# A macaron block (experts, state-space scan, experts): the order of work on both sides of the scans, split gathers, and two steps of scan 0 moved to GpSimd

## The reference

```
x = x + 0.5 * ffn(layernorm(x))
x = x + ssm(layernorm(x))
x = x + 0.5 * ffn(layernorm(x))        # same weights

ffn(x):  logits = x @ router_w                          # 8 experts
         e = argmax(logits); s = sigmoid(max(logits))
         out[t] = (silu(s*x[t] @ gate_w[e]) * (s*x[t] @ up_w[e])) @ down_w[e]
         out += (silu(x @ sh_gate) * (x @ sh_up)) @ sh_down      # every token
ssm(x):  dt_x, B, C = split(x @ W_x.T, [64, 16, 16]); dt = softplus(dt_x @ W_dt.T + b_dt)
         h[t] = exp(dt*A) * h[t-1] + dt*B*x;  y[t] = sum over 16 states of h*C;  y += x * D
```

## Time and profile before

| what | us |
|---|---|
| median of 3 runs (lowest, highest) | 548.02 (545.97, 550.7) |
| the profiled execution, its own time | 548.89 |
| its span, first to last instruction | 547.2 |
| busy: PE, DVE, ACT, POOL | 442.1 (81%), 342.6 (63%), 261.0 (48%), 277.4 (51%) |
| mean granted TensorE clock, of full speed | 0.921 |

### The profile page before, as it was taken

One profiled execution on the slowest core, in us unless ns is written; L12 is line 12 of the kernel. 1 busy time (PEld: TensorE's weight loads), 2 busy tenths in 40 slices (PEclk: granted clock), 3 DMA queues, 4 the chain that ended last, 5 costly groups with the idle time before them and its releaser, 6 DMA issues.

```text
span 547.2 us, 7087 instructions
## 1 busy us (share of the span) xinstructions
PE 442.1 (81%) x2236; PEld 308.7 (56%) x2236; DVE 342.6 (63%) x557; ACT 261.0 (48%) x499; POOL 277.4 (51%) x213
## 2 busy tenths in 40 slices
PE   1988899998777675796888688699789937999991
PEld 1855455554434465775775677689546523555550
DVE  5357244333665989998999899969757321333430
ACT  1200233331063899699899989767011001333330
POOL 6003266664120476688997989799200003466632
PEclk9869999999897999799799889879979985999997
DMA  8942022210410122131232133223041113132300
GB/s 291 383 123 65 21 77 62 67 47 20 153 60 0 42 77 78 59 108 49 91 100 94 44 101 100 83 62 104 1 136 58 54 63 82 57 93 84 112 30 8
DMA packets 33331, 45.69 MB, mean 84 GB/s; under 512 B 5258, under 2 KB 22478, under 8 KB 33296
## 3 DMA queue, kind: packets, MB, share of 16 engines
q1 hardware_dynamic: 28144, 34.70, 19.9%
q0 software_dynamic: 5152, 10.54, 6.6%
HBM read 37.33 MB, written 12.48 MB: 91 GB/s over the span
## 4 chain that ended last, share of the span: by engine, by line
PE 55%; DVE 23%; issue 9%; POOL 7%; ACT 3%; DMA 1%; DVEq 0%; POOLq 0%
PE bank L656 17%; DVE hs L1057 12%; PE bank L630 11%; PE bank L684 7%; PE bank L615 6%; POOL gs L378 3%; PE bank L770 3%; PE bank L585 2%; PE bank L753 2%; DVE stats L861 2%; DVE dbx_t L1041 2%; PE bank L672 2%; PE bank L667 2%; POOL xn_no L339 2%; PE bank L570 1%
## 5 line engine op out<-in xcount | busy, mean ns | idle before, releaser
L378 POOL TENSOR_TENSOR gs<-hs,c_sb 128x1024 f32<-128x1024 f32 x62 | 147.2, 2389 | 57.1 <-DVE hs L1057 50.6
L1057 DVE TENSOR_TENSOR_SCAN hs<-da,bank 128x1024 f32<-128x1024 f32 x64 | 145.1, 2277 | 4.7 <-PE bank L753 4.5
L753 PE MATMUL bank<-ident,dbx_t 128*128 128x128 f32 x512 | 74.0, 292 | 35.5 <-DVE hs L1057 32.4
L347 POOL DMA_INDIRECT da<-rows,row_token x46 | 47.3, 1029 | 102.2 <-DMA rows<-x_sb 55.9
L656 PE MATMUL bank<-w_gu,tt 128*128 x184 | 94.6, 638 | 3.9 <-ACT tt L434 3.9
L476 ACT ACTIVATE da<-dt_sb,a_neg 128x511 f32<-128x511 f32 x128 | 84.9, 712 | 13.8 <-DVE hs L1057 13.7
L753 PEld LDWEIGHTS bank<-ident,dbx_t 128*128 128x128 f32 x512 | 61.1, 150 | 49.3 <-DVE hs L1057 43.4
L490 ACT ACTIVATE dbx_t<-dtx_t,h_sb 128x256 f32<-128x256 f32 x194 | 83.7, 495 | 4.7 <-DVE dtx_t L1026 3.4
L967 DVE SCALAR_TENSOR_TENSOR q_sb<-th,bank 128x256 f32<-128x256 f32 x46 | 19.4, 421 | 103.4 <-ACT th L429 103.4
L770 PE MATMUL bank<-ident,gs 128*128 128x128 f32 x496 | 71.5, 292 | 8.2 <-POOL gs L378 8.0
L429 ACT ACTIVATE th<-bank,da 128x256 f32<-128x256 f32 x46 | 21.8, 474 | 102.8 <-PE bank L656 102.8
(11 more groups left out here) (118 smaller groups left out, 506.3 us busy)
## 6 DMA issues: line engine op xcount, KB each, us to landing
c_sb<-c_dram SPq DMA_DIRECT2D x64, 256.0 KB, 3.1
rows<-xn_no SPq DMA_DIRECT2D x8, 516.0 KB, 6.1
x_sb<-in_x SPq DMA_DIRECT2D x4, 512.0 KB, 6.4
w_gu<-in_gate_w SPq DMA_DIRECT2D x2, 1024.0 KB, 10.1
w_gu<-in_up_w SPq DMA_DIRECT2D x2, 1024.0 KB, 11.2
w_dn<-in_down_w SPq DMA_DIRECT2D x2, 1024.0 KB, 10.5
xn_no<-token_out SPq DMA_DIRECT2D x4, 512.0 KB, 6.3
rows<-x_sb SPq DMA_DIRECT2D x4, 512.0 KB, 3.5
```

Source lines behind the costliest of these rows:

```text
L347: nc.gpsimd.indirect_dma_start(out=xr[:, u, 0:WIDE[r]], out_offset=None, in_=rows[r], in_offset=bass.IndirectOffsetOnAxis(ap=row_token[:, ...
L378: nc.gpsimd.tensor_tensor(gs[:, s % 2], hs[:, s % RING], c_sb[:, s % RING].unsqueeze(1).to_broadcast([P, KC, L]), ALU.mult).then_inc(sc_g, 1)
L753: mm = nc.tensor.transpose(DBX[s % 2][:, k, i * P:(i + 1) * P], dbx_t[:, s % TURNS, i, k * P:(k + 1) * P], ident[:])
L1057: nc.vector.tensor_tensor_scan(hs[:, s % RING].rearrange(flat), da[:, s % RING].rearrange(flat), DBX[s % 2][:, :, :].rearrange(flat), 0.0, ...
```

## The change

It does the following, by place.

- XR is 7; BY_DVE of batch 3 and ROUTES are other values; three of the four route calls of run 1 stand in scan 3.
- Before the scans: the order of statistics, combines and normalisations on VectorE; normalise(1,2) on GpSimd; both shared_gate_up of batch 3 together, the second with its own banks and its hidden rows in y_sb's memory; shared_down(0,3), the transposes of batch 1's second half, and project(1) between turn_dbx calls and in the first scan step; its two shared_result halves after scan steps 1 and 2.
- In scan 0: combine(3) on GpSimd after product 4, rstd and normalise(1,3) there after product 9. Projection steps of batch 1 one state later, project(2) earlier.
- In scan 3: normalise(2,2) on VectorE. The last product but one on GpSimd, the last on VectorE in two halves.
- Behind the scans: the order of the shared expert, its down product into YA, count and sequence in other banks.
- Run 1's rows: SyncE writes the normalised rows to rows[0] and to rows[1], x_sb to rest and to rows[1]. The first seven tiles gather from rows[0], and later from rest; the others from rows[1]. result(0) to result(6) wait for the second gather.

```diff
...
-    XR = 6
+    XR = 7
...
-      + ((1, 1, 2, 1, 1, 1, 1, 1, 0, 1, 1, 1, 1, 0, 1, 1),))
-    ROUTES = (5, 10)
+      + ((1, 1, 2, 1, 1, 1, 1, 0, 1, 1, 1, 0, 1, 1, 1, 1),))
+    ROUTES = (4, 8, 13)
...
 def shared_banks(r, b, fo):
...
-    return (H[0], H[1]) if fo == 0 or (r, b) == (0, BATCH - 1) else (T, Y)
+    return (H[0], H[1]) if fo == 0 else (YS[0], YS[1]) if r == 1 or b == 3 else (T, Y)
...
+def hidden_rows(r, b):
...
+    return sg_h if (r, b) == (0, 3) else sh_h[:, b % 2]
...
+def shared_out(r, q):
...
+    return YA[q % 2] if r == 1 or q // 2 == 3 else YS[q % 2]
...
     def xn_rows(r):
...
-            sp.dma_start(row_tiles[r][:, rows_of(b), 0:D + 2], xn_no[:, rows_of(b), :]).then_inc(xn_out, 16)
+            sp.dma_start(row_tiles[0][:, rows_of(b), :], xn_no[:, rows_of(b), :]).then_inc(xn_out, 16)
+        for b in range(BATCH if r == 1 else 0):
+            sp.dma_start(row_tiles[1][:, rows_of(b), 0:D + 2], xn_no[:, rows_of(b), :]).then_inc(rows_full, 16)
...
     def rest_rows(b):
...
-        sp.dma_start(row_tiles[1][:, rows_of(b), D + 2:], x_sb[:, rows_of(b), :]).then_inc(rest_out, 16)
+        sp.dma_start(rest_tiles[:, rows_of(b), :], x_sb[:, rows_of(b), :]).then_inc(rest_out, 16)
+        sp.dma_start(row_tiles[1][:, rows_of(b), D + 2:], x_sb[:, rows_of(b), :]).then_inc(rows_full, 16)
...
     def experts(r):
...
-        def gather(j):
+        def gather(j, lo, hi, source, done):
...
-                out=xr[:, u, 0:WIDE[r]], out_offset=None, in_=rows[r],
+                out=xr[:, u, lo:hi], out_offset=None, in_=source,
...
-                bounds_check=TOK - 1, oob_is_err=False).then_inc(ff_in[u], 16)
+                bounds_check=TOK - 1, oob_is_err=False).then_inc(done[u], 16)
...
+        for j in range(XR):
+            gather(j, 0, WIDE[0], rows[0], ff_in)
+        if r == 1:
...
-        for j in range(XR):
-            gather(j)
+            for j in range(XR):
+                gather(j, WIDE[0], WIDE[1], rest, rest_in)
+            pool.wait_ge(rows_full, 16 * 2 * BATCH)
...
-                gather(j + XR)
+                gather(j + XR, 0, WIDE[r], rows[r], ff_in)
...
+    def combine(b):
+        pool.wait_ge(sh_x, LT // 2 * (b + 1))
+        pool.wait_ge(back_in[b], 16)
+        tiles = slice(LT * b, LT * (b + 1))
+        nc.gpsimd.tensor_tensor(x_sb[:, tiles], xn[:, tiles], x_sb[:, tiles], ALU.add).then_inc(back_x, 1)
...
     def scan(b):
...
-            if last_two(s):
+            if last_one(s):
...
-            if n == 3:
-                if b == 0:
-                    rstd_of(1, BATCH - 1)
-                else:
-                    rstd_of(2, b - 1)
+            if b == 0 and n == 4:
+                combine(BATCH - 1)
+            if b == 0 and n == 9:
+                rstd_of(1, BATCH - 1)
+                normalise(1, BATCH - 1)
+            if b > 0 and n == 3:
+                rstd_of(2, b - 1)
+                if b < BATCH - 1:
...
+    normalise(1, BATCH - 2)
...
     experts(1)
-    for u in range(4):
-        pool.wait_ge(ff_out[u], 16 * uses(u) * RUNS)
...
-            if more and n == 0:
+            if b == 1 and n == 0:
+                ln_copy(1, 7)
+            if more and b != 1 and n == 0:
...
-            if more and n in (1, 2):
-                project_abs(b + 1, n - 1)
-            if more and n == 3:
+            late = int(b == 0)
+            if more and n in (1 + late, 2 + late):
+                project_abs(b + 1, n - 1 - late)
+            if more and n == 3 + late:
...
-            if more and n == 4:
+            if more and n == 4 + late:
...
-            if n in (13, 14):
-                ln_copy(*((1, 6 + n - 13) if b == 0 else (2, 2 * (b - 1) + n - 13)))
+            if b == 0 and n == 14:
+                project_copy(2)
+            if b == 0 and n == 15:
+                ln_copy(1, 6)
+            turn = 13 if more else 10
+            if b > 0 and n in (turn, turn + 1):
+                ln_copy(2, 2 * (b - 1) + n - turn)
...
-    shared_tanh(0, 3, 0)
+    project_ln(0)
+    for fo in range(KC):
+        shared_tanh(0, 3, fo)
...
-    project_ln(0)
-    shared_tanh(0, 3, 1)
-    ln_copies(1, 2)
...
-    for s in range(AHEAD):
+    ahead(0)
+    ln_copy(1, 4)
+    for s in range(1, AHEAD):
...
+    ln_copy(1, 5)
...
+    for fo in range(KC):
+        shared_tanh(1, 0, fo)
+    shared_tanh(1, 1, 0)
...
     route(1)
-    for b in range(BATCH):
+    shared_tanh(1, 1, 1)
+    for b in range(2, BATCH):
...
     routed(1)
...
-                pe.wait_ge(pj_dtx, 4)
+                pe.wait_ge(pj_copy, 3)
...
     def route(r, b):
...
-            pe.wait_ge(sc_dve, states_by("dve", min(N * (BATCH - 1) + (ROUTES + (N, N))[b] + 3, STATES)))
+            pe.wait_ge(sc_dve, states_by("dve", min(N * (BATCH - 1) + (ROUTES + (N,))[b] + 3, STATES)))
...
-    def shared_down(r, b):
+    def shared_down(r, b, halves=(0, 1)):
...
-        if b == 0:
-            pe.wait_ge(rt_read, r + 1)
+        if (r, b) == (0, 0):
+            pe.wait_ge(rt_read, 1)
...
-        for q in range(2 * b, 2 * b + 2):
-            if q >= 2:
+        if (r, b) == (0, 3):
+            pe.wait_ge(pj_dtx, 2)
+        elif (r, b) == (1, 0):
+            pe.wait_ge(sc_x, KC * BATCH)
+        for q in (2 * b + h for h in halves):
+            if q >= 2 and (r, b) != (0, 3):
...
-                    last = nc.tensor.matmul(YS[q % 2][:, i * D:(i + 1) * D], sh_h[:, b % 2, k, t * P:(t + 1) * P],
+                    last = nc.tensor.matmul(shared_out(r, q)[:, i * D:(i + 1) * D], hidden_rows(r, b)[:, k, t * P:(t + 1) * P],
...
     def shared_gate_up(r, b, fo):
-        if b > 0:
-            pe.wait_ge(sh_hidden, 2 * (BATCH * r + b - 1) + fo + 1 + (fo if (r, b) == (0, BATCH - 1) else 0))
+        if (r, b, fo) == (0, 3, 1):
+            pe.wait_ge(sh_x, 6)
+        elif (r, b) == (1, 0):
+            pe.wait_ge(sc_h, STATES - 1 + fo)
+        elif b > 0:
+            pe.wait_ge(sh_hidden, 2 * (BATCH * r + b - 1) + fo + 1)
...
-    def shared(r, batches):
...
     def routed(r):
...
-            pe.wait_ge(ln_xnT, (GT // 2 + 6, GT, GT + 2)[b - 1])
+            pe.wait_ge(ln_xnT, (GT // 2 + 6, GT // 2 + 6, GT + 2)[b - 1])
...
+        if (b, k) == (2, 0):
+            pe.wait_ge(ln_xnT, GT)
...
-            pe.wait_ge(sh_hidden, 2 * BATCH)
+            pe.wait_ge(sh_hidden, 7)
...
-            pe.wait_ge(sh_x, GT // 2)
+            pe.wait_ge(sh_hidden, 8)
...
     def add(s):
...
-        products = gs
-        if last_two(s):
-            products = last
-            pe.wait_ge(sc_last, s - (STATES - 3))
-        else:
-            pe.wait_ge(sc_g, s + 1)
...
-            pe.wait_ge(pj_dtx, 2)
+            pe.wait_ge(sh_x, GT // 2)
...
+        if not last_one(s):
+            pe.wait_ge(sc_g, s + 1)
...
+            if last_one(s):
+                pe.wait_ge(sc_last, k + 1)
+            products = last if last_one(s) else gs[:, s % 2]
...
-                mm = nc.tensor.matmul(YA[k][:, i * P:(i + 1) * P], products[:, s % 2, k, i * P:(i + 1) * P], ident[:],
+                mm = nc.tensor.matmul(YA[k][:, i * P:(i + 1) * P], products[:, k, i * P:(i + 1) * P], ident[:],
...
+            if s == 0:
+                shared_down(0, 3, (1,))
+                ln_transposes(1, 5)
+                project(1)
+            if last_one(s):
+                shared_gate_up(1, 0, 0)
...
-            if more and n in (0, 1):
-                project_z(b + 1, n)
+            late = int(b == 0)
+            if more and n in (late, late + 1):
+                project_z(b + 1, n - late)
...
-            if n in (12, 13):
-                ln_transposes(*((1, 6 + n - 12) if b == 0 else (2, 2 * (b - 1) + n - 12)))
-            if n == N - 1 and b + 2 < BATCH:
+            turn = 12 if more else 9
+            if b > 0 and n in (turn, turn + 1):
+                ln_transposes(2, 2 * (b - 1) + n - turn)
+            if (b, n) in ((0, 13), (1, N - 1)):
...
+            if b == 0 and n in (14, 15):
+                ln_transposes(1, n - 8)
...
     route(0, BATCH - 1)
-    shared(0, 2)
+    count(0)
+    shared_gate_up(0, 0, 1)
+    shared_gate_up(0, 1, 0)
+    shared_down(0, 0)
+    sequence(0)
+    shared_gate_up(0, 1, 1)
+    shared_down(0, 1)
     routed(0)
...
-    shared_gate_up(0, 3, 0)
-    ln_batch(1, 1)
...
-    shared_gate_up(0, 3, 1)
-    ln_batch(1, 2)
-    shared_down(0, 3)
+    for fo in range(KC):
+        shared_gate_up(0, 3, fo)
+    ln_transposes(1, 2)
...
-    for s in range(2):
-        turn_dbx(s)
-    project(1)
+    ln_transposes(1, 3)
+    turn_dbx(0)
+    ln_transposes(1, 4)
+    turn_dbx(1)
+    shared_down(0, 3, (0,))
...
-    pe.wait_ge(sc_h, STATES)
-    route(1, 2)
-    shared_gate_up(1, 0, 0)
-    ln_batch(2, BATCH - 1)
+    shared_gate_up(1, 0, 1)
+    shared_gate_up(1, 1, 0)
+    ln_transposes(2, 6)
+    shared_down(1, 0, (0,))
+    ln_transposes(2, 7)
+    shared_down(1, 0, (1,))
     route(1, BATCH - 1)
-    shared(1, BATCH)
+    shared_gate_up(1, 1, 1)
+    count(1)
```

(85 more changed lines are left out.)

## The result

| | before | after |
|---|---|---|
| median (lowest, highest), us | 548.1 (545.97, 550.7), 4 runs | 515.64 (514.57, 515.98), 4 runs |
| profiled execution, its span | 548.89, 547.2 | 515.98, 514.3 |
| mean granted TensorE clock | 0.921 | 0.953 |
| busy PE, DVE, ACT, POOL, us | 442.1, 342.6, 261.0, 277.4 | 429.1, 339.3, 260.1, 292.7 |

The ratio is 0.9402 (95%: 0.9359 to 0.9446). The forecast was 514.2. The total came out near it by luck in part: the largest wrong term, 5.9 us, was offset by four small ones the other way, so the parts are what to read.

The account below looks back on a forecast made before the run. VectorE was taken to bound scan 0, TensorE the stretch behind the scans, work order the transition between. +0.4 - 8.7 - 0.9 - 21.7 - 3.8 = -34.7 us from 548.89 gave 514.2, range 505 to 526.

Parts of the forecast that it names:

- the 8.7: Transition and scan 0, up to scan 18: 8.7 us gained, scan 18 starting at 234.8 against 243.50.
- less some 8.5 of waits, 5.3 for ScalarE and 3.2 for GpSimd: Up to scan 18: waits taken off the 14 us earlier start plus 3.25 of VectorE's net work, leaving 8.7.
- the early lead is eaten by ScalarE: Rival, up to scan 18: only VectorE's lighter work gains, 0 to 4 us; total 519 to 523; chance 0.18.
- Scan 0's norm on GpSimd: Normalise(1,3) behind GpSimd's product 9: rstd 1.2 plus 4.84 us, products 10 to 15 then at 2.34 each.
- Scan 3: Batch 2's normalisation moves from GpSimd to VectorE, bank waits go, route calls fit beside scans: -0.9 us.
- the long figure: Scan 3: the moved normalisation costs VectorE 3.41 us beside products, taken as 3.4, rather than 1.37.
- Behind the scans: TensorE's shared work ends 46.0 us after the last scan, one idle piece of 1.1 us; first expert transpose 21.7 us earlier.
- the second rival: The join does not close: late residual gather or low TensorE clock behind the scans; 520 to 524 us; chance 0.17.
- The gather and the clock: Run 1's first tiles: no gather wait; without the gap, 3.19 us per tile at once, saving 3.8 us.
- T+57: Run 1's fourth tile: result(0) comes 57 us after the last scan's end; the residual gather lands at T+54.7.
- the 2.3 us of the prediction: Run 1's first tiles: spare time between the residual gather's landing and result(0).
- The 0.4 of the memset: Start: seven slots instead of six lengthen GpSimd's first memset, VectorE waits behind it: +0.4 us.

Follow-up runs that it names:

- run 1: Not a follow-up run: the kernel's own routed-expert pass behind the scans, 23 tiles, whose rows are gathered; no separate measured time.
- The old front kernel: Changed kernel with the transition into the scans and scan 0 as in the kernel before; 519.67 us, ratio 0.9476.
- the order alone: Kernel before with only scan 3 and the order behind the scans changed, one gather per tile in run 1; 530.41 us, ratio 0.9698.
- The one-gather kernels: Changed kernel, run 1 gathering whole rows once after all of x_sb is written; 525.04 us, ratio 0.9559; again on another chip 525.27, ratio 0.9605.
- the one with the transposes ahead: Changed kernel with the LayerNorm 1 transposes ScalarE waits for put ahead of turn_dbx(0) and turn_dbx(1); 510.24 us, ratio 0.9283.
- the split alone: Kernel before with only the split gathers and seven slots; 534.37 us, ratio 0.9748.

## Why the prediction was right, and where it was not

*The front: the 8.7 was mis-sized.* It measured 2.8 us in the profile, 2.5 to 4.1 by the experiments. The prediction called itself wrong where scan 18 moves by much other than 8.7, and in this term it was wrong. The first scan's lead was right (168.22 for 169.0; 12.9 us once run 0's 1.9 is taken off, for 14). The step that failed is "less some 8.5 of waits, 5.3 for ScalarE and 3.2 for GpSimd". From the first scan to scan 18 VectorE waited 14.2 us (1.6 in the kernel before). The part behind GpSimd's block was right, 3.3 us (2.29, 0.60 and 0.45); the part ahead of it measured 10.9 (2.06, 0.99, 2.91 and 4.94). I had named the two transposes that ScalarE waits for, but priced them at 1.4 and 3.7 with TensorE at its full clock. They cost 2.93 and 5.63, since the down product half between them took 3.44 instead of 1.89, turn_dbx(0) 1.94 instead of 1.07, and the transposes behind it 1.06 instead of 0.60: with the 1.22 instead of 1.07 of turn_dbx(2) this low clock, for which the forecast had no term, is 3.0 of the 3.5 us that the two waits were too long. A third wait was missing in the forecast, 4.94 for the turn of B (1.42 before). In TensorE's queue it stands behind the second z product (which waited 1.23 for ScalarE's late copy), a turn of dbx, an add and the skip product. Moving the transposes ahead gave back 7.8 us in the profile. That shows that the order of the queue was the cause, in part by way of the clock. The rival "the early lead is eaten by ScalarE" priced this stretch at 0 to 4 us, and 2.8 came; but ScalarE did not set the pace by its own work, it stood 8.6 us for the two transposes. Its total, 519 to 523, did not come, since the other terms made up for the front.

*Scan 0's norm on GpSimd.* The timeline of GpSimd, answering to the earlier trace rows:

```profile
194.05 2.19 POOL L393 TENSOR_TENSOR x_sb<-xn_no,x_sb 128x1024 f32<-128x1024 f32 x1
...
215.06 4.83 POOL L355 TENSOR_SCALAR xn_no<-x_sb,mv,rstd 128x256 f32<-128x256 f32 x4
```

It took 4.83 us for 4.84, the combine 2.19 for 2.4, with one wait of 2.29 and two short ones behind it. Its price was predicted rightly, though not how it comes about: the prediction let the products follow at 2.34 us each, and it came to TensorE's low clock (1.97 and 1.92 us at 222.26 and 224.02) after the 3.03 us that TensorE stood for the block. That the move made no difference against VectorE was not said. That the block can be cut up at the same work of GpSimd, and that this with the earlier statistics pays 4.4 us, was in no rival.

*Scan 3: better than predicted.* 2.2 us for 0.9. The old front kernel has the changed scan 3 and reaches T 327.37 us after F against 329.10 before: 1.7; with the order alone it is 2.4. The waits for banks in scans 1 to 3 fell from 4.5 us to 0.44, for 2.4 us more of VectorE's work (136.3 busy for 133.9). The normalisation took less than the long figure:

```profile
351.46 2.73 DVE L935 TENSOR_SCALAR xn_no<-x_sb,mv,rstd 128x256 f32<-128x256 f32 x4
...
354.98 2.29 DVE L1119 TENSOR_TENSOR_SCAN hs<-da,bank 128x1024 f32<-128x1024 f32 x1 [0.44 <-PE bank L791]
```

The Trainium skill's page "SBUF — State Buffer" ("Who interferes with whom") makes the two engines take turns by whole instructions, and the trace agrees: of the four instructions one took 1.76 us, from 351.46 to just behind the end of GpSimd's product at 353.07, and the others 0.40. In the 3.41 of before, one took 2.46 and the others 0.39 to 0.40. So what this work costs beside products is what is left of one product when it starts; the prediction had only the two totals.

*Behind the scans: right.* 46.93 us for 46.0, with the one idle piece of 1.1 us where it was put (1.08 before 388.07). The granted clock of 1.00 in all 33 us closes the second rival: the 0.74 of before did not belong to this work. In the kernel before TensorE had been busy 10.6 of the 15 us ahead of it, and had stood 1.68 us just before. The Trainium skill's page "TensorE: Matmul & The Clock Gate" ("HAM oscillation"), which lays the low clock to gaps between matmuls, had spoken against that rival, and here the trace agrees: no gap over 1.1 us, no fall. The rival's own price, 2.4 + 3.8 and 1 to 4, adds up to 521.4 to 524.4 and not to 520 to 524.

*The gather and the clock: right.* No wait for either gather; result(0), predicted at T+57, came at 436.26, T+57.3, without one. The margin was thinner than the 2.3 us of the prediction: the first residual gather was issued at 431.47, T+52.5, and with the 3.7 us of the earlier trace rows it would land at 435.2, an estimate of 1.1 us ahead of result(0). The tiles took 4.4 us less for 3.8. The one-gather kernels show that this part depends on the execution: 1.5 to 4.

*What no term held.* Start to F was 1.9 us shorter, although only a memset changed there. The 0.4 of the memset came (one of ScalarE's copies in the first LayerNorm starts at 14.43 for 14.04), and TensorE's clock outweighed it. The time to F goes either way in kernels that are alike there: 56.7 to 56.9 us in six of the fourteen profiles, 54.0 to 54.9 in the others. The same routes took:

```profile
25.80 3.64 PE L627 MATMUL bank<-w_rt,xnT 128*128 128x8 f32 x32
```

```profile
25.45 6.83 PE L627 MATMUL bank<-w_rt,xnT 128*128 128x8 f32 x32
```

The first is the changed kernel, the second the one with the transposes ahead; before had 6.83 too. The last 0.9 us, behind the last tile, are no chance. This piece took 14.0 us in the kernel before, 14.6 with the split alone, 13.1 to 13.2 in every profile with the changed order and the split, and 12.6 in the three with the order but one gather. So the split costs 0.5 to 0.6 there and the rest of the change gives 1.4 to 1.5. That rest took four waits out at the end of GpSimd's queue, which may be the cause; no run changes them alone.

So the sum missed by only 1.8 us because errors offset each other: 5.9 too much in the front and 0.9 behind the scans stood against 2.3 ahead of F, 1.3 in scan 3, 0.6 of clock and 0.9 at the end. That was luck; the 2.3 ahead of F above all is the clock of the one execution that was profiled.

## What to carry to other kernels

When work is moved forward into a queue, price the wait of whoever needs the last piece of it, not only the work's own time: two groups of transposes of 0.6 us each cost 8.6 us of ScalarE's time because they stood behind work that nobody needed as soon. Put what another engine's copy needs first, and cut a block of helper work into pieces near the slack of one step (here the pieces and a better place for the statistics came together). Where rows are gathered in a loop with an early and a late half, gather the early half as soon as its indices are there: the gap it closes is worth its length for certain, and the clock behind it only sometimes.

## What the runs showed of the hardware that was not expected

- The granted clock in the same instructions differs between executions: 32 route matmuls took 3.64 or 6.83 us, and with a gap of 8.6 to 9.0 us in front, the first two gate-ups of run 1 took 3.77 or 3.78 us each in three of the profiles (the kernel before, the first with one gather, the order alone), but 3.52 and 1.98 in the second with one gather.
- VectorE's last product, whose inputs are both in SBUF, runs as two halves. The row below has 2.19 us for both, but they are not alike: the first took 1.59 us and the second 0.68. GpSimd's last product ran from 377.66 to 380.01 us, beside the first alone. In the kernel before, the full width with none beside it took 2.33 us for two. So the first half lost about 0.9 us while GpSimd worked and the second nothing. Whether the shared port does it was not tried:

```profile
378.98 2.19 DVE L1147 TENSOR_TENSOR dbx_t<-hs,c_sb 128x512 f32<-128x512 f32 x2
```
